# Placing most tokens for the expert layer during the batch stage ahead of it, in a hybrid attention, mixing and expert kernel on one Trainium2 core

## The reference

```python
scores = jax.nn.softmax(x @ gate_w.T, axis=-1)
top_scores, sel = jax.lax.top_k(scores, K)
sel_flat = sel.T.reshape(-1)
order = jnp.argsort(sel_flat, stable=True)
tok_sorted = order % N
counts = jnp.bincount(sel_flat, length=E)
x_sorted = x[tok_sorted]
y = _grouped_swiglu(x_sorted, counts, w1, w2, w3)
weighted = y * scores_sorted[:, None]
out = jnp.zeros((N, D), x.dtype).at[tok_sorted].add(weighted)
```

## Time and profile before

| | |
|---|---|
| median of 3 runs | 1508.67 us (1508.36 to 1511.19) |
| the profiled execution | 1512.73 us, span 1510.8 us |
| granted TensorE clock, mean | 0.930 |
| PE busy | 1328.5 us, 88% (weight loads 1131.9 us, 75%) |
| DVE busy | 902.8 us, 60% |
| ACT busy | 670.5 us, 44% |
| POOL busy | 611.9 us, 41% |
| DMA | 157.83 MB, mean 104 GB/s |

### The profile page before, as it was taken

One profiled execution on the slowest core, in us unless ns is written; L12 is line 12 of the kernel. 1 busy time (PEld: TensorE's weight loads), 2 busy tenths in 40 slices (PEclk: granted clock), 3 DMA queues, 4 the chain that ended last, 5 costly groups with the idle time before them and its releaser, 6 DMA issues. The chain is left out here.

```text
span 1510.8 us, 27687 instructions
## 1 busy us (share of the span) xinstructions
PE 1328.5 (88%) x7528; PEld 1131.9 (75%) x7529; DVE 902.8 (60%) x2122; ACT 670.5 (44%) x1506; POOL 611.9 (41%) x561
## 2 busy tenths in 40 slices
PE   4999993889999999834899999998657899999996
PEld 3888993778888888722677778877556688888885
DVE  4777885534444444448889999984163344444442
ACT  3466763323333333234687676864332233333332
POOL 3667651245555555412132322222112455555553
PEclk9899995799999999967999999999858999999998
DMA  6475764256666433360000000000034567663332
GB/s 217 145 273 190 274 220 169 71 138 161 163 165 156 81 49 56 43 205 0 1 15 30 14 14 28 28 29 29 28 130 99 122 151 163 159 162 54 56 56 32
DMA packets 100872, 157.83 MB, mean 104 GB/s; under 512 B 10256, under 2 KB 60688, under 8 KB 100816
## 3 DMA queue, kind: packets, MB, share of 16 engines
q1 hardware_dynamic: 73120, 118.67, 23.4%
q0 software_dynamic: 27264, 37.82, 16.2%
q10 hardware_dynamic: 432, 0.66, 0.2%
HBM read 95.89 MB, written 61.21 MB: 104 GB/s over the span
## 5 line engine op out<-in xcount | busy, mean ns | idle before, releaser
L1055 DVE TENSOR_TENSOR second_hT_lo<-bank,second_hT_hi 128x512 fp32r<-128x512 f32 x71 | 49.1, 692 | 179.7 <-ACT second_hT_hi L937 179.7
L1055 DVE TENSOR_TENSOR first_hT_lo<-bank,first_hT_hi 128x512 fp32r<-128x512 f32 x71 | 49.1, 692 | 166.4 <-ACT first_hT_hi L937 166.4
L156 PE MATMUL bank<-second_ring,second_xT_hi 128*128 x284 | 121.5, 428 | 18.0 <-issue 15.8
L903 POOL DMA_INDIRECT out_x<-second_block_hot,second_add_token x53 | 84.0, 1585 | 123.8 <-ACT second_block_hot L945 47.2
L903 POOL DMA_INDIRECT x_rows<-first_block_hot,first_add_token x53 | 84.0, 1585 | 111.9 <-ACT first_block_hot L945 56.3
L156 PE MATMUL bank<-first_ring,first_xT_hi 128*128 x284 | 120.4, 424 | 6.6 <-issue 4.4
L157 PE MATMUL bank<-second_ring,second_xT_hi 128*128 x284 | 114.0, 401 | 0.0
L158 PE MATMUL bank<-second_ring,second_xT_lo 128*128 x284 | 113.7, 400 | 0.0
L157 PE MATMUL bank<-first_ring,first_xT_hi 128*128 x284 | 113.4, 399 | 0.0
L158 PE MATMUL bank<-first_ring,first_xT_lo 128*128 x284 | 113.1, 398 | 0.0
L1749 PE MATMUL bank<-b_fv,b_hT 128*128 128x256 f32 x480 | 107.0, 381 | 0.0
(11 more groups left out here) (344 smaller groups left out, 3991.5 us busy)
## 6 DMA issues: line engine op xcount, KB each, us to landing
first_ring<-split_weights SPq DMA_DIRECT2D x96, 256.0 KB, 3.1
second_ring<-split_weights SPq DMA_DIRECT2D x96, 256.0 KB, 3.2
a_wraw<-in_L_ffn_w SPq DMA_DIRECT2D x24, 512.0 KB, 6.4
split_weights<-a_whi SPq DMA_DIRECT2D x24, 512.0 KB, 2.7
split_weights<-a_wlo SPq DMA_DIRECT2D x24, 512.0 KB, 4.0
normed_rows<-xg SPq DMA_DIRECT2D x16, 528.0 KB, 3.1
x_rows<-x SPq DMA_DIRECT2D x8, 512.0 KB, 7.0
x<-x_rows SPq DMA_DIRECT2D x8, 512.0 KB, 7.3
```

The lines of the kernel that those rows point to most:

```text
L156: nc.tensor.matmul(out, hi, other_hi, start=start, stop=False)
L903: nc.gpsimd.indirect_dma_start(x_dram[:], bass.IndirectOffsetOnAxis(ap=add_token[q][:], axis=0), y[q], None, compute_op=ALU.add).then_inc( ...
L1055: nc.vector.tensor_tensor(hT_lo[par][:].rearrange("p k t -> p (k t)"), th_bank[par][:], hT_hi[par][:].rearrange("p k t -> p (k t)").bitcas ...
```

## The change

A token row's place needs only the counts of the tiles ahead. The change sorts the tokens of the first 6 batches (EARLY = 6 groups, TE = 24 tiles) while the last batch is still in attention (or mixing), and the last 2 groups (TL = 8 tiles) right after the last search, in the same phase. In the mixing four of the early groups stand in the last period, two behind it.

- *Regions.* When the early tokens are placed, the final first blocks of the experts are not known. So each expert gets a region of rows of an intermediate table: as many blocks as its early tokens need, and 8 more. The table of 120 rows (RB), one for each block of a region, stands in one PSUM bank (`place_tokens`; the operands are swapped against before). At the end `final_places` works out, for each of the 120 rows, to which final block it goes (`spot`, 120 x 72), and one matmul (`order_tokens`) moves the rows to their block and turns the table round. `row_token`, `end` and `base` are handed over to the expert phase (`Placed`), which starts with the columns of `row_token`.
- *Buffers.* All buffers of the placement lie on tiles of the phase that are dead by then (`Shelf`, `overlaid`). In attention `block_hot` has 2 buffers, `row_hot` and `sent` 3; in mixing 6, 3 and 6. The `y` outputs of the expert phase, before on dead placement buffers, are tiles of their own.
- *Ring.* The ring of weights is one tensor of the whole program, at the address of `x`: its slot 0 lies under the batches 0 to 5 of x. SP loads expert 0 into it (`first_in`) at the end of attention or mixing, when x of batches 0 to 6 has been stored, and ahead of the last batch's stores. Expert 1 comes at the expert phase's start: two pieces at once, four after `xt_done` has counted the first transposes. From expert 2 on the pieces are paced as before, with `floor` lowered from base 1 - 6 to 2 - 12.
- *Products in unread banks.* `keep_busy` issues 512-column matmuls into a bank that nobody reads: 12 before the last gate transposes of attention; 12 before and 4 after those of the mixing; 16 at the start of each expert phase, after `first_in`; 16 in front of the first `time_product` of the mixing, which thereby waits for the evacuation of projections, `fk_hi` and the chain's `num`.
- *Order in attention's last batch.* `weight_low` 0 and 1 stand ahead of the search of batch 6's logits, and the placement's steps take their places (`early_bases`, `early_places`).

The diff, cut to its core:

```diff
+CH = 4
+GROUPS = T // CH
+EARLY = GROUPS - 2
+TE = EARLY * CH
+TL = T - TE
+RB = TE * TOPK + EX - 1 + EX * TL + 1
...
+def keep_busy(nc, out, stationary, moving, times):
+    for _ in range(times):
+        nc.tensor.matmul(out, stationary, moving, start=True, stop=True)
...
+def hot_blocks(nc, dve, r, const, n):
+    depth = len(r.block_hot)
+    if n >= depth:
+        dve.wait_ge(r.sent_ready, n - depth + 1)
+    shape = [P, TOPK, CH, RB]
+    nc.vector.tensor_tensor(r.block_hot[n % depth], r.block_at[:, :, n * CH:(n + 1) * CH].unsqueeze(3).to_broadcast(shape),
+                            const.lane[:, 0:RB].unsqueeze(1).unsqueeze(1).to_broadcast(shape),
+                            ALU.is_equal).then_inc(r.block_hot_ready, 1)
...
+def send_tokens(nc, act, r, const, n):
+    depth = len(r.sent)
+    act.wait_ge(r.block_hot_ready, n + 1)
+    if n >= depth:
+        act.wait_ge(r.sent_used, n - depth + 1)
+    for j in range(CH):
+        t = n * CH + j
+        last = nc.scalar.activation(r.sent[n % depth][:, :, j, :], r.block_hot[n % len(r.block_hot)][:, :, j, :], ACT.Copy,
+                                    scale=const.token[:, t:t + 1])
+    last.then_inc(r.sent_ready, 1)
...
+def final_places(nc, own, r, const):
...
+    own.link(nc.vector.scalar_tensor_tensor(out=r.scored, in0=r.moved, scalar=1.0, in1=r.home, op0=ALU.mult, op1=ALU.mult,
+                                            accum_out=r.dest))
+    nc.vector.tensor_scalar(r.spot, const.blocks[:], r.dest, const.lane_of[:, 0:1], ALU.subtract, ALU.is_equal).then_inc(r.spot_ready, 1)
...
+def place_tokens(nc, pe, r, n):
+    pe.wait_ge(r.row_hot_ready, n + 1)
+    pe.wait_ge(r.sent_ready, n + 1)
+    for k in range(TOPK):
+        for j in range(CH):
+            last = nc.tensor.matmul(r.region_bank[0:RB, 0:P], r.sent[n % len(r.sent)][:, k, j, :], r.row_hot[n % len(r.row_hot)][:, k, j, :],
+                                    start=n == k == j == 0, stop=n == GROUPS - 1 and k == TOPK - 1 and j == CH - 1)
+    last.then_inc(r.sent_used, 1)
...
+def order_tokens(nc, pe, r):
+    pe.wait_ge(r.region_ready, 1)
+    pe.wait_ge(r.spot_ready, 1)
+    nc.tensor.matmul(r.table, r.region[0:RB, :], r.spot[0:RB, :], start=True, stop=True).then_inc(r.table_done, 1)
...
             over_batches(sp, period)
+            sp.wait_ge(x_stored, 16 * (B - 1))
+            for piece in range(PIECES):
+                load_expert(sp, ring, w_split, 0, piece, first_in)
             store_x(B - 1)
             store_rows(B - 1)
...
             over_batches(act, period)
+            send_tokens(nc, act, route, const, 0)
             route_before(B)
+            send_tokens(nc, act, route, const, 1)
             gate_rows(B)
+            send_tokens(nc, act, route, const, 2)
+            send_tokens(nc, act, route, const, 3)
             gate_logits(B)
+            send_tokens(nc, act, route, const, 4)
             row_exp(B)
+            send_tokens(nc, act, route, const, 5)
             row_finish(B)
...
+                if is_last(b):
+                    dve.wait_ge(top_taken, B - 2)
+                    early_choices(nc, placing, route, idx, const)
                 if not is_first(b):
                     dve.wait_ge(x1_ready, 2 * b)
                     statistics(bn2, mv2, b - 1, var2_ready)
+                if is_last(b):
...
+                if is_last(b):
+                    weight_low(b, 0)
+                    weight_low(b, 1)
                 if not is_first(b):
                     softmax_begin(b)
-                weight_low(b, 0)
+                if is_last(b):
+                    early_bases(nc, placing, route, const)
+                else:
+                    weight_low(b, 0)
...
-                weight_low(b, 1)
+                if is_last(b):
+                    early_places(nc, placing, route)
+                else:
+                    weight_low(b, 1)
...
             over_batches(dve, period)
             own.round(B + 1)
+            positions(nc, placing, route, slice(0, TE))
+            hot_blocks(nc, dve, route, const, 0)
             dve.wait_ge(x1_ready, 2 * B)
             statistics(bn2, mv2, B - 1, var2_ready)
+            hot_rows(nc, dve, route, const, 0)
+            for n in range(1, EARLY):
+                hot_blocks(nc, dve, route, const, n)
+                hot_rows(nc, dve, route, const, n)
             softmax_begin(B)
...
             softmax_end(B)
+            late_places(nc, dve, placing, route, const)
+            for n in range(EARLY, GROUPS):
+                hot_blocks(nc, dve, route, const, n)
+                hot_rows(nc, dve, route, const, n)
+            final_places(nc, placing, route, const)
+            row_tokens(nc, dve, placing, route, const)
             own.pad()
...
             over_batches(pe, period)
+            place_tokens(nc, pe, route, 0)
+            pe.wait_ge(v_ready, 2 * B)
+            pe.wait_ge(var2_ready, B)
+            keep_busy(nc, q2[:], xnT_hi[1][:, 0, 1:P + 1], xnT_hi[1][:, 0, 1:N + 1], 12)
             gate_transposes(B)
+            place_tokens(nc, pe, route, 1)
             gate_products(B)
+            for n in range(2, EARLY - 1):
+                place_tokens(nc, pe, route, n)
+            count_choices(nc, pe, route, const, 1)
+            for n in range(EARLY - 1, GROUPS):
+                place_tokens(nc, pe, route, n)
+            order_tokens(nc, pe, route)
...
+            for piece in range(2):
+                load_expert(sp, ring, w_split, 1, piece, slot_in[1])
+            announce(0)
+            sp.wait_ge(xt_done, 1)
+            for piece in range(2, PIECES):
+                load_expert(sp, ring, w_split, 1, piece, slot_in[1])
+            announce(1)
+            sp.wait_ge(pace_ready, 1)
+            for n in range(2, EX):
                 for piece in range(PIECES):
...
-            nc.gpsimd.iota(floor[:], pattern=[[PIECES, EX], [1, PIECES]], base=1 - PIECES, channel_multiplier=0,
+            nc.gpsimd.iota(floor[:], pattern=[[PIECES, EX], [1, PIECES]], base=2 - 2 * PIECES, channel_multiplier=0,
...
-            nc.vector.tensor_tensor(pace[:, 1:EX, :], endb[0:1, 0:EX - 1].unsqueeze(2).to_broadcast([1, EX - 1, PIECES]),
-                                    paced[:, 1:EX, :], ALU.min).then_inc(pace_ready, 1)
+            nc.vector.tensor_tensor(pace[:, 2:EX, :], endb[0:1, 1:EX - 1].unsqueeze(2).to_broadcast([1, EX - 2, PIECES]),
+                                    paced[:, 2:EX, :], ALU.min).then_inc(pace_ready, 1)
...
+            pe.wait_ge(first_in, 32 * PIECES)
+            keep_busy(nc, y_bank[:], const.ones[:], ring[:, 0, 0, 0:H], 16)
...
             pe.wait_ge(w_in, 64)
+            pe.wait_ge(kvr_evac, 6)
+            pe.wait_ge(fk_hi_ready, 1)
+            pe.wait_ge(num_ready, 1)
+            keep_busy(nc, xb_[4][:], fk_hi[:, 0, 0:P], fk_hi[:, 0, 0:N], 16)
             time_product(0)
...
             over_periods(pe, period)
+            for n in range(EARLY):
+                place_tokens(nc, pe, route, n)
+            pe.wait_ge(fs_ready, 2 * B)
+            pe.wait_ge(varg_ready, B)
+            keep_busy(nc, xb_[4][:], fk_hi[:, 0, 0:P], fk_hi[:, 0, 0:N], 12)
             gate_transposes(B - 1)
+            keep_busy(nc, xb_[4][:], fk_hi[:, 0, 0:P], fk_hi[:, 0, 0:N], 4)
             gate_products(B - 1)
+            count_choices(nc, pe, route, const, 1)
+            for n in range(EARLY, GROUPS):
+                place_tokens(nc, pe, route, n)
+            order_tokens(nc, pe, route)
```

## The result

The changed kernel takes 1454.01 us, the median of 4 runs (1450.92 to 1456.09), against 1509.23 us for the kernel before beside it. The ratio is 0.962, 95% interval 0.9601 to 0.9639: 3.8% faster. The profiled execution took 1455.75 us (span 1454.0), 56.98 us less than the profiled one of before; forecast were 56.9. The two medians are 55.2 us apart, and 1452 was forecast for the one of the changed kernel.

The account below looks back on a forecast made before the run. It took TensorE at 2.4 GHz to bound the loops, with losses at the starts and in weight gaps; -9 - 18.5 - 26.9 - 2.5 = -56.9 from a 1508.67 us median gives 1451.8 us (forecast 1452), range 1440 to 1468.

Parts of the forecast that it names:

- The first start: From attention's last batch to block 1 of the first expert phase: -9 us, bounds -3 to -15.
- The masking: In attention's last batch: added rank and place steps on VectorE make the masking 2.1 us late.
- The way to the search: Attention's end, masking to last logits' search: six early groups of masks ahead; search at 251.5, 6.9 us later in all.
- The way from the search to block 1: End of attention into the first expert phase: 25.9 us in place of 42.7, -16.8.
- Weights: Expert loops: earlier loading of experts 0 to 2 removes three gaps of 6.4, 11.1 and 9.4 us: -26.9.
- Second start: End of mixing to block 1 of the second expert phase: early placement work hidden, -18.5 us, bounds -13 to -21.
- Mixing's start: First 16 output products of the mixing run at full clock after 16 warming products: -2.5 us, at most -2.66.
- (1): Both starts: the clock stays at half despite warming products, costing 12 us: 1464; chance 9%.
- (2): Attention's end: early masks, port and double buffers delay the last batch by what is saved later: 1461; chance 13%.
- (3): Expert phase starts: gathers queue behind expert 1's pieces, 2 to 3 us each, part hidden: 1455; chance 7%.
- (4): Expert loops: each block itself grows; 0.40 us more per block would cancel the gain; chance 2%.
- (5): Expert loops: a new gap at expert 2 or later, queue held by expert 1's wait: +5, 1457; chance 7%.

Follow-up runs that it names:

- old pace: Changed kernel with the pace's offset as before, so expert 2's weight pieces are let in at 7 to 12 blocks, not 2 to 7: 1462.39 us.
- early scaling: Changed kernel, attention's end reordered: groups 1 and 2 scaled before the last rows' normalisation, group 4 before the logits, 8 warming products, not 12: 1456.57 us.
- tightened's second and third form: Changed kernel with both starts reordered, 6 warming products before attention's gate transposes, 13 (second) or 16 (third) at each expert phase's start: 1454.43 and 1452.0 us.
- late masks: Changed kernel with attention's six early groups (masks, scalings, products) behind the last search instead of before it: 1459.58 us.

## Why the prediction came out right

**The first start was right in its sum and wrong in its parts.** Forecast -9, measured -9.44 from the start of the span to block 1's first product. But 4.01 us of it came in attention's first seven batches, before any step of the placement runs, and that was luck. Without them the start has gained 5.43 us, not 9 to 9.9, though inside the bounds of -3 to -15. The search at 250.84, where 251.5 was forecast, is the same luck: counted from the masking of the 7th batch it is 10.2 us late, not 6.9.

Three steps were mis-sized. The masking: forecast 2.1 us late, measured 3.42. (The terms written out for it, 1.4 + 1.35 + 1.35 - 1.14 - 1.2, make 1.8.) The weight part moved ahead was priced at 1.2 us; the two that now stand there take 5.34 us (214.79), beside an addition of GpSimd's that takes 3.22 (215.84) and 2.37 in the kernel before, where a weight part alone takes 1.22. That this is the missing time was not tested. The way to the search: 4.8 us forecast, 6.82 measured. Of the 2.0 us 0.7 lie between the masking and the output step (2.66 us in place of 1.95). TensorE now stands waiting for the masking, and its last products of attention run partly at half clock, before and after:

```profile
225.77 2.02 PE L757 MATMUL bank<-a_kvb,a_qr 128*128 128x128 f32 x16
```
```profile
225.15 3.53 PE L1075 MATMUL bank<-a_kvb,a_qr 128*128 128x128 f32 x16 [3.03 <-DVE a_kvb L941]
```

The granted clock from 225 to 229 us is 0.59. With the same stop of 3.03 us the run with the old pace keeps its clock (2.05 us). For the rest, the step that failed is GpSimd's chain, for which I allowed "1 to 2 us more, mostly behind the warming products". It needs 5.5 us from 234.76 to 240.25 where the same four steps beside no mask take 1.9, at this place in the kernel before and in the end of the mixing. ScalarE, which stood at the normalisation for it, had group 1's scaling behind that. That stopped VectorE for 3.74 us, and the run with early scaling took 2.35 of them back. The way from the search to block 1: -15.67 in place of -16.8. Of the 1.1 us 0.8 lie before the phase's start (15.02 us where 14.2 were summed) and 0.3 behind it (12.01 for 11.7): the 16 products were 0.5 us quicker than counted, and the gather, which I had behind them, leaves TensorE standing for 0.55 us. Beside the loads of expert 1 it takes 4.97 us from its issue to the transposes, and 3.13 without them in the kernel before.

**The 4 us in attention's first batches** were in no term. 0.3 is when the program got going. The other 3.7 lie between the first search after 60 us and the masking of the 7th batch: 131.22 us in both traces of the kernel before's attention, 127.54 and 127.55 in the three of the changed one and 127.53 to 127.61 in its nine variants, with the same instructions in the same order. So they belong to the program and come with every execution; luck is only that the forecast missed the rest by as much. VectorE and GpSimd in the batch behind 70 us, of before and of after (L590 and L875 are the same weight part, L496 and L779 the same addition of the bias to x):

```profile
70.58 2.36 POOL L496 TENSOR_TENSOR x<-x,a_lepe_bias 128x1024 f32 x1
...
70.95 3.07 DVE L590 TENSOR_TENSOR a_wlo<-a_wraw,a_whi 128x1024 fp32r<-128x1024 f32 x1
```
```profile
70.62 3.45 POOL L779 TENSOR_TENSOR x<-x,a_lepe_bias 128x1024 f32 x1
...
70.63 1.21 DVE L875 TENSOR_TENSOR a_wlo<-a_wraw,a_whi 128x1024 fp32r<-128x1024 f32 x1
```

In before GpSimd starts first and VectorE's instruction, 1.22 us alone, needs 3.07; in after both start within 0.01 us, VectorE's passes in 1.21 and GpSimd's needs 3.45 in place of 2.36. The masking in this batch comes 1.7 us earlier, and TensorE's wait for it (0.64 us) and for the next batch's operand (0.76) is gone. The other 2.0 us are won two batches on, and the same pair stands there: in before GpSimd starts at 121.73, 0.11 us ahead, and VectorE needs 3.32; in after they start 0.02 us apart (119.74), and VectorE passes in 1.21. Both batches go the slow way in both traces of before's attention, with 26.3 to 26.6 us from masking to masking, and the quick way in all twelve of the changed kernel and its variants, with 24.3 to 24.8. The Trainium skill, "SBUF — State Buffer", section "Who interferes with whom", says that of such a pair the one that issues first has the shared port for its whole instruction and the other waits; the trace agrees where the starts lie 0.37 and 0.11 us apart, and at 0.02 us and less it does not tell which was first. What in the change moved VectorE's step by 0.1 to 0.4 us is not shown. That this collision accounts for the 3.7 us is read from two batches of each trace; no run turned the order round on its own. Nor does it always cost: in the 7th batch of four variants (no warming products, early scaling, tightened's second and third form) VectorE's step needs 3.34 to 3.36 us in the same way, and the batch is only 0.1 us longer than in the others.

**Weights.** -26.9 forecast, -25.07 measured from block 1 to block 70 in both phases. The gaps were as forecast (27.0 in the run that has this part alone, 9.98 for the third by the old pace), and 1.7 us of the difference is the slightly slower block. "Blocks 4.86 us apart" was 4.88, against a mean of 4.870 in before.

**Second start.** -18.5 forecast, -17.24 measured to block 1's activation. Up to the end of the last logits' product it is -2.19 (forecast -2.65), from there to block 1's product 26.53 us (forecast 25.7, although the terms written out add up to 25.0): again the gather, for which TensorE waits 0.8 us, and small steps.

**Mixing's start.** -2.5 forecast; the products themselves gave 6.28 - 3.72 = 2.56. Not forecast are 1.73 us between the last block and this place and 0.5 at the end; the first stretch took 67.2 to 68.5 us in the traces of the changed kernel and its variants, against 68.94 and 71.57 in the two of before's, so some of it is spread between executions.

**The rivals.** (1) The half clock through the starts: does not hold. It is at half until the phase starts (0.50 from 250 to 266 us, as the 0.23 us for a product of the placement had it), but full in block 0; the run without warming products lost 9.3 us of the 12 that it was priced at. (2) falls by the run with the late masks. (3) holds in part: 1.8 us more for the gather, of which TensorE stands for 0.55 and 0.8 us at the two starts of the first trace (0 to 1.0 in the other two), where 2 to 3 were named. (4) holds in kind and not in size: 0.012 us for a block in place of 0.40. (5) falls.

## What to carry to other kernels

Work that is moved ahead into a busy phase is free only as far as its engine stands idle there, and a third engine's queue can take part of that away. The mixing covered all 13.2 us of masks. Attention's end, where VectorE would stand for 10 us, covered 5.7; the order of ScalarE's queue, a scaling behind a normalisation, was worth 2.35 of the rest. When a stage is shortened, look at what it had covered (here 3 MB of weights, 26.6 us at the two starts), and price a burst of loads by its bytes at the rate that the trace shows, not by the issues. And compare two traces by marks inside them: a sum that fits to a tenth held 4 us that nobody had forecast.

## What the runs showed of the hardware

- An instruction on VectorE and one on GpSimd of 128x1024 that start within 0.4 us of each other cost one of them 1.1 to 2.1 us: GpSimd 3.45 in place of 2.36, or VectorE 3.07 and 3.32 in place of 1.22. GpSimd's four steps on four numbers took 5.5 us beside VectorE's masks and 1.9 without. Two such pairs that fell the other way go with 3.7 us over attention.
- After 13 products and 1.29 or 0.84 us of standing still (the two starts of tightened's second form), block 0 ran at half clock (0.63 us a product) until 270.4 and 1093.1; after 16 products and 0.55, 0.8 or 1.00 us it did not.
- The same stop of 3.03 us at attention's end left the next 16 products at full clock in one run (old pace, 2.05 us) and partly at half in another (3.53).
- From the last block of a loop of four to the next the interval is 0.08 us longer than the others and the one behind it 0.08 shorter, in before and after alike; in one kernel and one phase of it, whose loop is the same, it is 0.23 us longer, and 0.15 of that is lost.
